# An attention block on one core: projections moved between the tiles of the heads, output projection moved into a last stage

## The reference

```
q, k, v = xf @ Wq.T, xf @ Wk.T, xf @ Wv.T        # each head, 1024 -> 64
s = where(mask, q @ k.T / 8, min);  p = softmax(s);  o = p @ v
out = x + concat(o).reshape(B, 2048, 1024) @ Wo.T
```

## Time and profile before

| what | us |
|---|---|
| median of 3 runs | 3385.69 (3383.26 to 3387.61) |
| the profiled execution | 3385.93 |
| its span, first to last instruction | 3383.9 |
| PE busy | 3176.5 (94%) |
| DVE, ACT, POOL busy | 2068.3, 1740.5, 1672.6 |
| mean granted clock of TensorE | 0.986 |

### The profile page before, as it was taken

How to read it: one execution, slowest core, us unless ns; L and a number is a source line. 1 busy time by engine, 2 the same in 40 slices (tenths; PEclk the granted TensorE clock), 3 DMA queues, 4 the chain that set the end, 5 groups by cost and what they waited for, 6 DMA issues and landing times.

```text
span 3383.9 us, 50389 instructions
## 1 busy us (share of the span) xinstructions
PE 3176.5 (94%) x14472; PEld 2494.5 (74%) x14472; DVE 2068.3 (61%) x3454; ACT 1740.5 (51%) x3525; POOL 1672.6 (49%) x1306
## 2 busy tenths in 40 slices
PE   4999998999999679999999999999999999999998
PEld 3888887788888457777777777777777777777776
DVE  6212111310110488888888888888888888888885
ACT  2100110210100267777767777777777777777774
POOL 2000000100000367777777777777777777777774
PEclk9999999999999789999999999999999999999999
DMA  6325223422311222111112111212121112111210
GB/s 236 100 84 137 93 66 82 154 71 50 97 62 48 65 83 62 59 55 44 56 50 69 44 56 50 69 44 57 51 69 44 51 56 68 45 50 57 64 37 19
DMA packets 142546, 232.91 MB, mean 69 GB/s; under 512 B 76800, under 2 KB 76800, under 8 KB 142336
## 3 DMA queue, kind: packets, MB, share of 16 engines
q1 hardware_dynamic: 142336, 230.73, 22.8%
HBM read 163.58 MB, written 67.11 MB: 68 GB/s over the span
## 4 chain that ended last, share of the span: by engine, by line
PE 28%; POOL 13%; DVE 12%; issue 9%; ACT 1%; DMA 1%; POOLq 0%; DVEq 0%; SPq 0%; ACTq 0%
POOL p_low L690 6%; POOL k L715 4%; PE acc L1059 4%; PE acc L1063 4%; PE max L1015 4%; PE acc L1061 4%; PE scores L1045 4%; PE rows L1077 3%; PE scores L1040 3%; DVE o_full L984 3%; DVE part_max L930 2%; POOL q L711 2%; DVE p_low L690 2%; DVE diagonal L701 1%; PE side L1025 1%
## 5 line engine op out<-in xcount | busy, mean ns | idle before, releaser
L690 POOL TENSOR_TENSOR p_low<-probs,p_high 128x512 fp32r<-128x512 f32 (+2 forms) x960 | 1190.9, 1258 | 573.8 <-ACT p_high L863 539.9
L859 ACT ACTIVATE probs<-scores 128x512 f32<-128x512 f32 (+3 forms) x1280 | 684.3, 535 | 410.0 <-PE scores L1045 383.6
L930 DVE TENSOR_REDUCE part_max<-max 128x1 f32<-128x512 f32 (+3 forms) x1280 | 766.1, 603 | 197.8 <-PE max L1015 175.8
L863 ACT ACTIVATE p_high<-scores 128x512 fp32r<-128x512 f32 (+3 forms) x1280 | 683.4, 534 | 0.0
L1015 PE MATMUL max<-k,q 128*128 128x512 f32 (+3 forms) x1280 | 489.5, 383 | 72.6 <-DVE part_max L930 36.0
L1059 PE MATMUL acc<-p_high,v 128*128 128x512 f32 (+3 forms) x1280 | 477.6, 373 | 28.3 <-POOL p_low L690 20.1
L318 DVE COPY stage_d<-proj 128x512 f32<-128x512 f32 x96 | 66.0, 690 | 710.9 <-PE proj L264 462.7
L1040 PE MATMUL scores<-q,k 128*128 128x512 f32 (+3 forms) x1280 | 478.0, 373 | 11.9 <-ACT p_high L863 8.9
L1045 PE MATMUL scores<-q,k 128*128 128x512 f32 (+3 forms) x1280 | 489.0, 382 | 0.0
L1063 PE MATMUL acc<-p_low,v 128*128 128x512 f32 (+3 forms) x1280 | 469.0, 366 | 0.0
L1061 PE MATMUL acc<-p_high,v 128*65 128x512 f32 (+3 forms) x1280 | 462.2, 361 | 0.0
(11 more groups left out here) (96 smaller groups left out, 5083.5 us busy)
## 6 DMA issues: line engine op xcount, KB each, us to landing
raw<-qk_s SPq DMA_DIRECT2D x256, 256.0 KB, 4.2
xs<-xT SPq DMA_DIRECT2D x64, 512.0 KB, 5.0
w_raw<-wqk SPq DMA_DIRECT2D x32, 512.0 KB, 3.7
qk_s<-stage_a SPq DMA_DIRECT2D x64, 256.0 KB, 2.4
qk_s<-stage_d SPq DMA_DIRECT2D x64, 256.0 KB, 2.4
raw<-v_s SPq DMA_DIRECT2D x64, 256.0 KB, 2.8
res<-x_res SPq DMA_DIRECT2D x32, 512.0 KB, 4.4
out<-res SPq DMA_DIRECT2D x32, 512.0 KB, 2.6
```

What stands on the lines that cost most here:

```text
L690: eng.tensor_tensor(p_low[:, n % 4, part], probs[:, n % 4, part], p_high[:, n % 4, part].bitcast(F32), ALU.subtract).then_inc(done, 1)
L859: nc.scalar.activation(probs[:, n % 4, 0:cols], scores[n % 2][:, 0:cols], ACT.Exp, scale=SCALE).then_inc(exp_done, 1)
L863: nc.scalar.activation(p_high[:, n % 4, 0:cols], scores[n % 2][:, 0:cols], ACT.Exp, scale=SCALE).then_inc(high_act, 1)
L930: nc.vector.tensor_reduce(part_max[:, s % 2, at, m:m + 1], max_bank[n % 2][:, 0:cols], AX.X, ALU.max).then_inc(max_read, 1)
```

## The change

There are now three functions.

**`begin`** does batch 0 only: the same two reads, but every split part is also stored (`store_x`) in new DRAM tensors `xh_s` and `xl_s`, in pieces of 256 tokens. It computes 32 tiles of 512 columns: q and k of pairs 0 and 1, and v of the eight LB heads of batch 0.

**`attend`** computes all other projections between its slots. A "unit" is 24 matmuls of 256 columns (one block of 256 tokens, one of q, k or v of one pair); pairs 2 and 3 have 16 units, pairs 4 to 15 have 24, 320 in all, 7680 matmuls. `filler` lays the units of a pair evenly over 80 slots (the two heads that run two pairs earlier): 7.2 matmuls a slot from head 4 to head 27, 4.8 in heads 2 and 3, 3.6 in heads 0 and 1, none in heads 28 to 31. Their inputs are streamed: 2 MB for each block, 112 blocks; weights 0.5 MB a set, split by ACT (L944) and POOL. A unit's bank is copied out by ACT one slot after it is full ("evict"); a unit of v is also turned by PE ("turn", two 128x128 transposes) and copied again ("turned out"). The banks `side` and `rows` become `spare0` and `spare1`; units, turns and shifts share them by the rule in `homes`. Batch 1's statistics and splits run in the slots of heads 2 to 9. The loops over pairs are unrolled. The output projection is gone from here: each head's result is stored in `o_s`.

**`finish`** loads and splits `Wo` and the 32 results and does the output projection, 1536 matmuls of 512 columns.

```diff
+def begin(nc, xT, wqkv, wv, xh_s, xl_s, qk_s, v_s):
+            for h in range(X_UNITS):
+                load_x(1, h)
+                if h >= X_SLOTS:
+                    store_x(h - X_SLOTS)
...
+def filler():
+    for pair in range(LEAD, PAIRS):
+        own = [u for u, unit in enumerate(every) if unit[0] == pair and u >= PRO_UNITS]
+        base, products = (pair - LEAD) * 2 * SLOTS, PRODUCTS * len(own)
+        for m, u in enumerate(own):
+            taken = {}
+            for k in range(PRODUCTS):
+                taken.setdefault(base + (m * PRODUCTS + k) * 2 * SLOTS // products, []).append(k)
+            for slot, ks in taken.items():
+                put(slot, "unit", u, ks[0], ks[-1] + 1)
+            finish[u] = slot
+    for u, slot in finish.items():
+        put(slot + 1, "evict", u)
+        put(slot + 2, "keep", u)
+        if every[u][2] == 2:
+            put(slot + 3, "turn", u)
+            put(slot + 4, "turned out", u)
...
+            load, high = ((-12, -4), (-2, 0), (2, 4))[c]
+            put(base + load, "w load", w)
+            put(base + high, "w high", w)
+            put(base + high + 1, "w low", w)
...
-                elif step == "project":
...
+            def spare_bank(*key):
+                n, earlier = home[key]
+                if earlier is None:
+                    return spare[n]
+                step, h, *last = earlier
+                if step == "unit":
+                    pe.wait_ge(evicted, h + 1)
+                elif step == "shift":
+                    pe.wait_ge(shift_ready, h * STAGES + last[0] + 1)
+                elif step == "turn":
+                    pe.wait_ge(v_ready, turns.index(h) + 1)
...
+                    if k0 == 0:
+                        pe.wait_ge(w_low, sets.index((pair, c)) + 1)
+                        pe.wait_ge(x_loaded[b % 2], 32 * (b // 2 + 1))
+                        to = spare_bank("unit", u)
...
+                    for m in range(k0, k1_):
+                        ch, w, x = products[m]
+                        last = nc.tensor.matmul(to[:, 0:BLK], w[:, c, ch, :],
+                                                x[:, b % 2, ch, :], start=(m == 0), stop=(m == PRODUCTS - 1))
...
+def finish(nc, x_res, wo, o_s, out):
```

More of the change, by code:

```diff
@@ L540, in attend @@
-def attend(nc, x_res, wo, qk_s, v_s, out):
+    plan = [("raw", 0, 0), ("raw", 0, 1), ("w load", 0), ("x load", 0)]
+    for n in range(SPLITS):
+        if n in (4, 8):
+            plan.append(("raw", 0, n // 2))
+        if n == 6:
+            plan += [("raw", 0, 3), ("w load", 1), ("x load", 1)]
+        plan += [(step, 0, n) for step in ("k2 high", "split high", "split low")
+                 if step != "k2 high" or n in K2_SLOT]
+        if n in (3, 7):
+            plan += [("w high", n // 4), ("w low", n // 4)]
@@ new lines, in prologue, with homes @@
+    plan += [("scores", 0, t) for t in range(AHEAD)]
+    plan += [("evict", u), ("keep", u)]
+    return plan
+def homes(steps):
+    home, left, owner, summing = {}, [-1, -1], [None, None], None
+    for at, (step, *which) in enumerate(steps):
+        if step not in ("unit", "shift", "turn", "gn mean", "gn spread"):
+            continue
+        key = (step, *which[:2]) if step == "shift" else (step, which[0])
+        if key not in home:
+            bank = min((n for n in range(2) if n != summing), key=left.__getitem__)
+            home[key] = bank, owner[bank]
+            owner[bank] = key
+        bank = home[key][0]
+        left[bank] = at
+        if step == "unit":
+            summing = None if which[2] == PRODUCTS else bank
+    return home
@@ new lines, in attend, with steps @@
+        gn_kept = sem("gn_kept")
+        every = units()
+        sets = weight_sets()
+        turns = [u for u, unit in enumerate(every) if unit[2] == 2]
+        stores = [u for u, unit in enumerate(every) if unit[2] < 2]
+        blocks = []
+        for unit in every:
+            if not blocks or blocks[-1] != unit[:2]:
+                blocks.append(unit[:2])
+        def steps():
+            yield from prologue()
+            for h in range(G_HEADS):
+                yield from slots(h)
+            for step in ("leave", "invert", "spread", "divide", "store"):
+                yield (step, G_HEADS - 1, 3)
@@ L780, in _, with wait_kept @@
+            def wait_kept(pair):
+                own = [m for m, u in enumerate(stores) if every[u][0] <= pair]
+                for slot in range(2):
+                    sp.wait_ge(kept_out[slot], 16 * sum(m % 2 == slot for m in own))
+                own = [u for u in turns if every[u][0] <= pair]
+                reached(sp, v_out, 16 * len(own))
+            for step in steps():
+                do(*step)
+            sp.wait_ge(o_stored, 16 * G_HEADS)
         @block.gpsimd
         def _(pool):
-            nc.gpsimd.memset(probs[:, 0, 0 * P:1 * P], 0.0).then_inc(eye_made, 1)
```

1251 lines of the change are left out of this document (735 added, 516 removed).

## The result

The changed kernel takes 3733.83 us (median of 4 runs, 3730.48 to 3736.24), the kernel before beside it 3386.65 (3383.26 to 3388.71): ratio 1.1026, 95% interval 1.1006 to 1.1045. It is slower by 347 us, where 107 were forecast. The profiled execution has a span of 3734.4 us.

A forecast was written before the change was run, and what follows sets the result against it. The prediction took PE's work plus 8.2 us of small stalls a head as the bound. Its seven stage terms (125, 130, 59, 293, 2282, 227, 375) sum to 3491, with 2 us around the span 3493 us; range 3330 to 3590.

The forecast's parts named there:

- Terms 1 to 3 and 7: First eight tiles 125 us, 24 further tiles 130, passage into the heads 59; `finish` and the end 375.
- Term 1: First eight tiles, with stores among the loads: end at 125 us, from 97 plus 25 for stores and 3 for clock.
- Term 3: From the last projection matmul to slot 0 of the first head: 59 us, where 49 pass before the change.
- the first reading: Heads of the kernel before: 60.0 us of PE work in 68.2, so filling could bring at most 262 us.
- term 5: Heads 4 to 27: 95.1 us each, 2282 in all, from PE's work, transposes, small stalls, bank waits and weights.
- term 6: Heads 28 to 31, without filling or output projection: 59 us each, 50 for the last, 227 in all.
- Bank waits: Heads 4 to 27: PE waits for ACT's spare-bank copies behind two exponentials, seven places, 9.1 us a head.
- Weights: Heads 4 to 27: PE waits for the next pair's weights through one buffer, 1.3 us a head, bounds 0 and 3.
- Term 4: Heads 0 to 3: 65.8 us for the first two, 71.5 for the next, plus stalls of 5 and 4: 293.
- Rival (a): Heads 4 to 27: bank waits hardly cost, 2.8 us a head, no wait for weights; kernel 3287 us, chance 0.22.
- (b): Heads: ACT is held by its loads, 4 us a head, 96 us more; kernel 3589 us, chance 0.14.
- (c): Narrow matmuls: weight loads bound them at 0.188 us, 545 us more; kernel 4038 us, chance 0.02.

The follow-up runs named there:

- b1: Kernel before the change, with 44 of the 48 output projection matmuls of every head left out: 3370.10 us against 3383.02.
- e1: Changed kernel, with ACT's copies out of the spare banks put ahead of the slot's exponentials: 3562.48 us.
- e2: Changed kernel, with the next pair's weight sets loaded and rounded earlier, for pairs after the first filled three: 3645.76 us.
- e3: Changed kernel with the edits of e1 and e2 together (also written e3_both): 3455.30 us.
- e5: On top of e3, the shift (PE's matmul and ACT's row copy) also put ahead of the slot's scores: 3428.15 us.
- e6: On top of e5, the group norm's pieces spaced further apart, with loads further ahead: 3415.54 us.
- e7_last_heads: On top of e6, DVE instead of POOL makes three of the ten low parts in heads 28 to 30: 3409.90 us.
- b5_dve_k: Kernel before the change, with two of the ten low parts, both of k, made by DVE instead of POOL in every head but the first: 3352.94 us.

## Why the prediction was wrong

The sign was right; the time was 241 us too low and outside the range.

- *Terms 1 to 3 and 7*: the sums held (312.7 for 314, 375.9 for 375), those of 1 to 3 by luck. Term 1 was 13 us too high: 111.7 is 97 and 15, close to the +14 of stores that use all idle time of the DMA engines (they moved 375 GB/s from 45 to 95 us, against 184 before), where +25 and +3 were taken. Term 3 was 12 us too low. `finish` cost its 347 us of matmuls and 29 of start, slow clock and end.
- *The failed step is the first reading*: "PE stands still for 8.2 us a head ... 32 x 8.2 = 262 us is what filling the heads could bring". It subtracted PE's work from the length and took the rest for idle time, all the free time there was, that filling takes away. Neither holds.
- *Not all of it is idle.* Between the starts of PE's matmuls in heads 10 to 27 of the kernel before, 59.4 us a head are the regular distances (0.228, 0.172, 0.117 and 0.057 us for 512, 384, 256 and 128 columns; a tenth of the starts are as close or closer), 5.3 are small excesses over these, none with an idle time of 0.15 us or more, and only 3.4 lie at longer stops. The small excesses stay in every form of the kernel: 5.4 in b1, 4.3 in the changed kernel, 4.4 or 4.5 in e1, e2, e3 and e5. "The old stalls mostly go, I leave 1.0" is this step in term 5: 3.3 us a head too little, some 80 us in 24 heads. Some are regular: behind the last scores matmul of a tile of 384 columns or fewer the next start is 0.05 us late in both kernels. No edit here answers to them, and what they come from stays open.
- *And what was idle was not all that was free.* Of PE's work, the output projection's 11 us were themselves in the shadow of the relay (b1: 10 of them worth 0.4 us a head). Taking them out of a head could bring next to nothing, while they cost their full price in `finish`. From this follow term 6 (59 taken within its bounds of 53 and 68.2; 67.6 measured; 29 us too low) and the wrong sense of "What goes: some 230 us of PE's stalls". The bound of 68.2 was in the text; the reason to take the low side ("DVE 53 without that stage's two additions and low parts") looked at totals of engines, when the row to read was ACT's wait of 146.3 us for raw inputs in the earlier trace rows, a relay that does not get shorter when PE has less to do.
- *Term 5 as a whole*, heads 10 to 27 of the changed kernel, 101.9 us against 95.1: regular distances 82.5 (83.7 forecast, with the transposes), small excesses 4.3 (1.0), stops 12.3 (9.1 for bank waits and 1.3 for weights), and 2.7 for matmuls at the lower clock, which the term did not have at all. e3_both has none of the last: its clock is 1.00 there. The signs of being wrong that the prediction named, heads under 90.6 us or less than 4 us of idle time before units, both looked for heads that are too short, so they stayed silent.
- *Bank waits*: mechanism and place right, price right for one (1.47 against 1.44 in the rows shown) and, a little high, for a head (7.5 listed against 9.1; the `v_kept` waits number 3.5 a head for the four counted). e1 and e5 take them away. They cost more than their listed length: e1 shortened heads 4 to 27 by 7.3 us each, while the waits that it removed make 6.1 (91.6 / 14.7, less the 2.4 / 15.8 that remain). Of the rest 0.7 is less time at the lower clock.
- *Weights*: mechanism right, size wrong: 3.6 us a head where 1.3 was taken with 3 as upper bound; e2 gives back 88 us, 3.7 a head. The bound had no place for the lower clock behind a stop of 3.4 us.
- *Term 4*: the stalls of 5 and 4 us a head were 12 in heads 0 and 1, 20 and 15 in heads 2 and 3: the same error, and 27 us of DVE's waits for the group norm's pieces, which the prediction did not price. e6 recovers 12 us or so.
- *Rival (a)*, cheap bank waits: not so, by e1. *(b)*, ACT held by its loads: it waited 1.5 us for raw k in 1500. *(c)*, weight loads bounding the narrow matmuls: these start 0.12 us apart (1511.36 and 1511.48) beside loads of 0.19:

```profile
L1181 PEld LDWEIGHTS spare<-block_high,block_wl 128*128 128x128 f32 x1409 | 274.4, 195 | 10.1
```

The rule that the prediction quotes from the Trainium skill (TensorE: Matmul & The Clock Gate, Part 3, The mechanism), that a load overlaps only for another row group, does not hold for these full loads. The same section also names a background weight buffer as a place into which a load is pulled ahead, and that way out the prediction left unmentioned.

What stays open: 24 us still separate e7_last_heads, the best form of the change, from the kernel before. A start of `finish` within heads 28 to 31, where PE has room, was not tried, and what the many small excesses come from was not looked for.

## What to carry to other kernels

Work that sits in another chain's shadow is nearly free; before pricing its removal, ask what the stretch would take without it, and if one can, leave the work out and time it (one run, b1, showed in a line what the busy shares hid). A length minus an engine's work is not idle time either: count the stops themselves. Where filling work reuses a bank, the copy that frees the bank belongs, in the copying engine's order, ahead of the work that the same slot has just issued to that engine: moving two lines was worth 171 us of 347. And an idle wait of a few microseconds on PE can be charged twice, once as the wait and once in the slower matmuls behind it (12.3 and 2.7 us a head in the changed kernel).

## What was not expected of the hardware

- After a stop of PE of 3.4 us the granted clock was at the lower level for the matmuls behind it (256 columns every 0.22 us instead of 0.12), with PE 89% busy from 1000 to 2500 us. After a single stop of 1.3 us (1511.16 and 1511.36, 0.20 apart, then 0.12) only the first distance was longer. But after two bank waits close together, 1.3 us before the matmul at 1331.66 and 1.5 before the one at 1334.90, the granted clock was 0.50 from 1334.5 to 1337.9 us, so short stops can cost it too.
- POOL takes 1.30 us for a low part of 64 partitions by 512 columns, as for one of 128 by 512 (1.29): half the partitions are no cheaper. DVE took 0.69 us for a part of k of 64 by 512 in b5_dve_k. From POOL's timeline of the changed kernel, and DVE's of b5_dve_k:

```profile
3181.65 1.30 POOL L737 TENSOR_TENSOR q<-raw,q 64x512 fp32r<-64x512 f32 x1
...
3192.40 1.29 POOL L728 TENSOR_TENSOR p_low<-probs,p_high 128x512 fp32r<-128x512 f32 x1 [1.34 <-ACT p_high L930]
```

```profile
2553.70 0.69 DVE L715 TENSOR_TENSOR k<-raw,k 64x512 fp32r<-64x512 f32 x1
```
